# One core, a Macaron block (two top-1 MoE layers around a circulant state-space layer): order of the w1 load and its centering, square roots through Ln and Exp, slot softmax ahead of the third expert's output copy, last expert's rows written straight into row form

## The chip, the cores and the metric

One core of one Trainium2 chip (trn2). The metric is the device time of one execution in microseconds (us). The kernel before took 154.5 us in the median of three runs (153.84 to 155.39).

## The reference

The input `x` is 8 x 512 tokens of 128 floats. `LN` is a layer norm without gain and bias, epsilon 1e-5.

```python
x = x + 0.5 * moe(LN(x))          # first pass
x = x + ssm(LN(x))
x = x + 0.5 * moe(LN(x))          # second pass

def moe(tokens):                  # 4096 tokens, E = 8 experts, F = 512, CAP = 160
    probs = softmax(tokens @ gate_w)
    expert = argmax(probs)
    pos = running count of the token within its expert; dropped when pos >= CAP
    return probs[expert] * (relu(tokens @ w1[expert]) @ w2[expert])   # 0 for a dropped token

def ssm(u):                       # per batch, state h of 128
    h_t = W h_(t-1) + B_w u_t     # W circulant, diagonal in the Fourier basis, |eigenvalue| 1
    return C_w h_t + D * u_t
```

## The kernel before

All arithmetic is float32 apart from the counting masks. The program has three stages, and five engines that run their own instruction lists and meet through semaphores.

**Head (0 to 32 us).** PE computes gate logits of all tokens from a transposed copy of x (`gate_turned`, `turn_logits`). DVE picks the expert of each token (`rate`, `choose`, L575 to L586), counts (`count_up`, L614), PE turns counts into ranks with three small matmuls (`rank`, L923 to L926), DVE makes one-hot tables (`number`, `encode`, `encode_place`, L630 to L656), and PE multiplies them, 32 matmuls of 20 columns (`place`, L934), which gives the list of tokens by slot (`index` on DVE, L664 to L671, tile `tok`). There are 8 x 160 = 1280 slots, in 10 tiles of 128. In between PE centers w1: the layer norm's mean is folded into the weights by a 128 x 128 product per expert (`center_w1`, L907, PSUM banks 0 and 1 in turn, copied back to `w1s` by ScalarE, L398). `keep_warm` (L863) are dummy bf16 matmuls of 512 columns. The constants, x, w1 and w2 come in one after the other on SyncE's queue (L265 to L277): w1 and w2 in halves, each half of w1 (1024 KB) followed by the same experts' w2.

**A MoE pass (`slots(n)`, first 32 to 61 us, second 117 to 153 us).** GpSimd issues ten gathers, one for each tile of slots (`gather`, L326), each row by token number. PE turns each gathered tile (step `i`, L949), ScalarE copies it to `xcT` (L406), and PE computes slot logits (`l`, L954), the first product of an expert (`u`, L965, four chunks in two halves, ReLU by ScalarE, L414) and the second (`d`, L976), which comes out transposed. DVE copies that to `eoT` (L705), PE turns it to rows (`o`, L985), DVE scales it by the slot's probability and adds the residual (`xnew`, L715), and GpSimd scatters the tile (L335). The probabilities need the variances of all ten tiles (`gmv`, L679), a root (`gsd`, L423, Sqrt), the reciprocal `grs` (L684), three DVE instructions to `lg`, an Exp (`prob_e`, L427) and three more DVE instructions to `gscale` (L694 to L696). Sqrt and Exp lie in different activation tables, so a table is loaded at L424 in each pass, ahead of the Exp, and one at L459 for the state-space stage.

The order inside a pass is written out by hand in three strings, one for each of PE, DVE and ScalarE: in `pe_steps` `u3` is expert 3's first product, in `dve_steps` `d2` its copy of expert 2's output, `l0` and `f0` the two halves of the softmax; in `act_steps` `g0` is the root, `e0` the Exp, `u` the ReLUs.

**State-space stage (61 to 108 us).** Eight batches go through a ring between ScalarE and PE: `normalise` (u, L466), `turn_u` (L1034), `copy_uT` (L453), `group_sums` (L1043), `turned_part` (vq, L445 and L446), and again `normalise` of the batch two further. Beside it DVE computes statistics (`stats`, L737 and L742), `shift` (L753 and L754) and the recurrence (va, z, zs, state), GpSimd two products of it. `deviation(b)` (L459, Sqrt) gives the standard deviation `ssd`, whose reciprocal `srs` DVE makes in `shift`; `ssd` itself scales the gate logits for the second pass (`gate_back`, L798). The second pass's ranks, places and index are computed in the last batches (L575 to L671 again), and its gathers wait for the index and for the last write of x2.

ScalarE's list at the start of this stage, and the layer norm's root:

```python
deviation(0); normalise(0); deviation(1); copy_uT(0); normalise(1); turned_part(0)
for i in range(NB):
    copy_uT(i + 1); deviation(i + 2); turned_part(i + 1); normalise(i + 2)
```

Of the kernel before, what the change touches and what calls it, by code (L numbers as in the profile page):

```python
# [5 lines left out]
def macaron_moe_ssm_kernel(nc, x_in, x_turned, a_params, b_w, c_w, c_w_turned, d_skip, gate_w, w1, w2,  # L6
# [40 lines left out]
    with ctx:  # L47
# [171 lines left out]
        gsd_r, lg_r, pe_r = (sem(n) for n in ("gsd_r", "lg_r", "pe_r"))  # L219
# [2 lines left out]
        svar, ssd_r, snb_r, u_r = (sem(n) for n in ("svar", "ssd_r", "snb_r", "u_r"))
# [30 lines left out]
        pe_steps = steps("i0 x1 i1 x2 u0 i2 l0 l1 d0 i3 u1 i4 u2 i5 d1 i6 l2 l3 i7 l4 l5 u3 i8 l6 l7 i9 l8 l9 d2 "  # L253
                         "u4 o0 o1 d3 u5 o2 o3 d4 o4 u6 o5 d5 u7 o6 d6 o7 d7 o8 o9")

        dve_steps = steps("i0 i1 i2 i3 i4 d0 i5 i6 i7 i8 d1 i9 l0 d2 f0 o0 o1 d3 p5 "
                          "o2 o3 d4 p6 o4 o5 d5 o6 d6 o7 d7 o8 o9")

        act_steps = steps("i0 i1 u0 i2 i3 u1 i4 u2 i5 i6 i7 u3 i8 i9 g0 e0 u4 u5 u6 u7")
# [928 lines left out]
```

## Time and profile before

| | |
|---|---|
| median of 3 runs | 154.5 us (153.84 to 155.39) |
| the profiled execution's own time | 155.39 us |
| its span, first to last instruction | 153.2 us |
| PE busy | 135.3 us (88%) |
| DVE, ACT (ScalarE), POOL (GpSimd) busy | 88.6, 57.4, 54.3 us |
| mean granted TensorE clock | 0.956 of full speed |
| half clock granted in | slices 6 and 7 of 40 (around 23 to 31 us), slice 30, and the end |

A matmul of float32 operands stands as two rows (two passes), so an expert's product of 4 chunks is "x8". PEld is the loading of stationary operands, which overlaps PE. In a row of the timeline the first number is the start, the second the time that it covers, then engine, line, operation, output and input tiles; `pair` is a PSUM pair of banks. In square brackets stands how long the engine was idle before it and who released it. SPq and POOLq are the instruction queues of SyncE and GpSimd. A span on POOL is rough.

### The profile page before, as it was taken

How to read it: one execution, taken by the hardware profiler on the slowest of the kernel's cores; microseconds unless marked ns; L12 is line 12 of the kernel's file. 1: busy time of each engine (PE TensorE's matmuls, PEld its weight loads, DVE VectorE, ACT ScalarE, POOL GpSimd, SP SyncE). 2: the span in 40 equal slices, each digit the busy share in tenths (PEclk: the TensorE clock that was granted, in tenths of full speed). 3: DMA queues.
4: the chain of work that ended last, by engine and by line, in shares of the span. 5: the costliest groups of instructions: out<-in, count | busy, mean ns of one | idle time of the engine just before them, and what ended most of it. 6: DMA issues, size and time to landing. Idle time of an engine off the chain costs nothing.

```text
span 153.2 us, 2526 instructions
## 1 busy us (share of the span) xinstructions
PE 135.3 (88%) x784; PEld 103.0 (67%) x784; DVE 88.6 (58%) x384; ACT 57.4 (37%) x141; POOL 54.3 (35%) x87
## 2 busy tenths in 40 slices
PE   5897999999999969579999999999979899999810
PEld 2324476368999946239888778878874399899700
DVE  1078796954446541276877978999882243554220
ACT  2513410444583406055564656451100145742200
POOL 3440000777205777101311221122002777027770
PEclk9999995599999999999999999999996999999995
DMA  4999999111100111690011011101011111001110
GB/s 121 282 357 386 369 486 415 39 51 51 34 0 17 58 51 54 199 327 28 0 68 45 23 73 68 70 1 68 4 68 68 51 51 51 21 0 51 54 51 17
DMA packets 11308, 16.21 MB, mean 106 GB/s; under 512 B 1664, under 2 KB 6272, under 8 KB 11264
## 3 DMA queue, kind: packets, MB, share of 16 engines
q1 hardware_dynamic: 9504, 13.11, 24.2%
q0 software_dynamic: 1280, 2.62, 5.5%
q10 hardware_dynamic: 512, 0.33, 0.9%
q8 instruction: 6, 0.10, 0.3%
q14 instruction: 6, 0.05, 0.1%
HBM read 12.65 MB, written 5.51 MB: 118 GB/s over the span
## 4 chain that ended last, share of the span: by engine, by line
PE 43%; issue 12%; DVE 11%; DMA 11%; POOL 10%; ACT 5%; SPq 4%; POOLq 1%; DVEq 0%
PE pair L965 9%; PE pair L976 7%; PE pair L907 7%; DMA w1s<-w 5%; POOL xg L326 4%; PE pair L1043 4%; ACT u L466 3%; SPq L267 2%; PE pair L934 2%; POOL out L335 2%; PE pair L863 2%; POOL x_scratch L335 2%; PE pair L1034 2%; DMA x<-x_scratch 2%; DVE sstat L737 2%
## 5 line engine op out<-in xcount | busy, mean ns | idle before, releaser
L863 PE MATMUL pair<-warm_in,ones_bf 128*128 128x512 bf16 x70 | 20.3, 437 | 3.3 <-DMA x<-x_scratch 1.7
L976 PE MATMUL pair<-hT,w2s 128*128 128x160 f32 x128 | 20.4, 302 | 0.2 <-ACT hT L414 0.2
L965 PE MATMUL pair<-xcT,w1s 128*128 128x160 f32 x128 | 20.5, 303 | 0.0
L414 ACT ACTIVATE hT<-pair 128x320 f32<-128x320 f32 x32 | 14.0, 438 | 15.2 <-PE pair L965 13.5
L965 PEld LDWEIGHTS pair<-xcT,w1s 128*128 128x128 f32 x128 | 18.0, 190 | 1.2 <-ACT xcT L406 0.8
L976 PEld LDWEIGHTS pair<-hT,w2s 128*128 128x128 f32 x128 | 17.9, 190 | 0.4 <-issue 0.2
L326 POOL DMA_INDIRECT xg<-x,tok x10 | 10.2, 1020 | 19.9 <-issue 19.9
L863 PEld LDWEIGHTS pair<-warm_in,ones_bf 128*128 128x128 bf16 x70 | 7.5, 112 | 13.1 <-issue 4.7
L326 POOL DMA_INDIRECT xg<-out,tok x10 | 10.1, 1012 | 13.6 <-DVE tok L671 10.8
L678 DVE BATCH_NORM_STATS2 gstat<-xg 128x6 f32<-128x128 f32 x20 | 5.8, 290 | 14.2 <-DMA xg<-out,tok 10.3
L335 POOL DMA_INDIRECT x_scratch<-xnew,tok x10 | 9.9, 993 | 10.8 <-DVE xnew L715 9.0
L335 POOL DMA_INDIRECT out<-xnew,tok x10 | 9.9, 990 | 9.4 <-DVE xnew L715 7.2
L356 POOL TENSOR_TENSOR vb<-vq,st 128x128 f32<-128x128 f32 x8 | 3.7, 458 | 25.9 <-ACT vq L446 25.9
L466 ACT ACTIVATE u<-x,snb,srs 128x128 f32<-128x128 f32 x28 | 11.6, 482 | 0.7 <-DVE snb L754 0.5
L406 ACT COPY xcT<-pair 128x128 f32<-128x128 f32 x20 | 5.3, 264 | 15.9 <-PE pair L949 15.8
L907 PE MATMUL pair<-w1s,center 128*128 128x512 f32 x16 | 10.5, 806 | 0.2 <-DMA w1s<-w 0.2
L705 DVE COPY eoT<-pair 128x160 f32<-128x160 f32 x16 | 5.1, 318 | 8.2 <-PE pair L976 8.2
L715 DVE SCALAR_TENSOR_TENSOR xnew<-pair,gscale,xg 128x128 f32<-128x128 f32 x20 | 6.4, 347 | 5.9 <-PE pair L985 5.9
L1043 PE MATMUL pair<-uT,vt 128*128 128x128 f32 x64 | 8.5, 276 | 0.9 <-ACT uT L453 0.9
L737 DVE BATCH_NORM_STATS2 sstat<-x 128x6 f32<-128x128 f32 x32 | 6.9, 278 | 3.8 <-DMA x<-x_scratch 3.8
L398 ACT COPY w1s<-pair 128x512 f32<-128x512 f32 x8 | 4.7, 586 | 11.6 <-PE pair L907 11.6
L1077 PE MATMUL pair<-gt,state 128*128 128x272 f32 x32 | 8.8, 396 | 0.0
(181 smaller groups left out, 245.0 us busy)
## 6 DMA issues: line engine op xcount, KB each, us to landing
xt<-x_turned SPq DMA_DIRECT2D x8, 256.0 KB, 5.9
w1s<-w SPq DMA_DIRECT2D x2, 1024.0 KB, 7.4
w2s<-w SPq DMA_DIRECT2D x8, 256.0 KB, 6.7
x<-x_scratch SPq DMA_DIRECT2D x8, 256.0 KB, 4.3
out<-x SPq DMA_DIRECT2D x8, 256.0 KB, 2.0
ce<-const_early ACTq DMA_DIRECT2D x1, 318.0 KB, 4.7
...
xg<-x,tok POOLq DMA_INDIRECT x10, 2.5
```

The source lines that it names most:

```text
L326: pool.indirect_dma_start(xg[:, j, :], None, (x_rows, out_rows)[n], bass.IndirectOffsetOnAxis(ap=tok[:, j:j + 1], axis=0), bounds_check=T ...
L335: pool.indirect_dma_start((x1_dram, out_rows)[n], bass.IndirectOffsetOnAxis(ap=tok[:, j:j + 1], axis=0), xnew[:, j, :], None, bounds_check ...
L414: nc.scalar.activation(hT[:, e % 2, half * HC:(half + 1) * HC, :], bank[4 + half][:, 0:HC * CAP] .rearrange("p (c s) -> p c s", c=HC), ACT ...
L466: ins = nc.scalar.activation(u[:, b % 2, c, :], x1[:, b * TB + c, :], ACT.Identity, bias=snb[:, b % 2, c:c + 1], scale=srs[:, b % 2, c:c + 1])
L715: V.scalar_tensor_tensor(xnew[:, i, :], bank[2 + i % 2][:, 0:P], gscale[:, i:i + 1], xg[:, i, :], ALU.mult, ALU.add).then_inc(row_sb, 1)
L737: ins = V.bn_stats(sstat[:, b % 2, c, :], x1[:, b * TB + c, :])
L863: M(bank[to][:, :], ones_bf[:, :], warm_in[:, :], start=True, stop=True)
L907: M(bank[e % 2][:, :], center[:, :], w1s[:, e, :], start=True, stop=True).then_inc(w1c_ps, 1)
L965: ins = M(bank[4 + half][:, c * CAP:(c + 1) * CAP], w1s[:, i, ch * P:(ch + 1) * P], xcT[:, i * CAP:(i + 1) * CAP], start=True, stop=True)
L976: ins = M(bank[6 + i % 2][:, 0:CAP], w2s[:, i, c, :], hT[:, i % 2, c, :], start=(c == 0), stop=(c == FC - 1))
L1043: ins = M(bank[5][:, 0:NG], vt[:, TB - 1 - c, :], uT[:, b % 2, c * P:(c + 1) * P], start=(c == 0), stop=(c == TB - 1))
L1077: ins = M(y[:, h, E:E + 2 * PITCH], state[:, b % 2, :], gt[:, 2 * h:2 * h + 2, :].rearrange("p r c -> p (r c)"), start=False, stop=True, s ...
```

## The change

1. SyncE issues both halves of w1 before all of w2.
2. On PE, experts 4 and 5 of w1 are centered ahead of `place(0, 0)`, experts 6 and 7 behind it. Eight `keep_warm` matmuls that stood ahead of `place` are gone.
3. Roots are taken as exp(0.5 ln v), and reciprocal roots as exp(-0.5 ln v), on ScalarE. One table with Ln and Exp is loaded at the start. The reciprocals of DVE at L684 and L753 are gone. The state-space stage has three activations for each batch instead of one.
4. In a pass `u3` goes behind `i9 l8 l9` on PE; `o0 o1` go ahead of `u4`; on ScalarE the root goes ahead of `u3`'s ReLUs, the Exp behind them; on DVE `f0` goes ahead of `d2`.
5. Expert 7's second product takes hT as the stationary operand and w2 as the moving one (step `t`), so it comes out in rows: `t8` (32 slots) and `t9` (128 slots) replace `d7`, DVE's copy of it, `o9` and a part of `o8`.
6. In `choose`, the last instruction writes `chosen` in its own order (expert, then tile) and reads `key` across.

```diff
             for i in range(2):
                 h = slice(i * E // 2, (i + 1) * E // 2)
                 sp.dma_start(w1s[:, h, :], w1[h].rearrange("e d f -> d e f")).then_inc(d_w1[i], 16)
+            for i in range(2):
                 for e in range(i * E // 2, (i + 1) * E // 2):
                     sp.dma_start(w2s[:, e, :, :], w2[e].rearrange("(c p) d -> p c d", p=P)).then_inc(d_w2[i], 16)
...
-            nc.scalar.activation(table_load[:, 0:1], eps[:, 0:1], ACT.Sqrt)
+            nc.scalar.preload_act_table_set("natural_log_exp_and_others")
...
-                        act.wait_ge(rated, n * NS + NS)
-                        nc.scalar.activation(gsd[:, :], gmv[:, :, 1], ACT.Sqrt, bias=eps[:, 0:1]).then_inc(gsd_r, 1)
-                        nc.scalar.activation(table_load[:, 1:2], eps[:, 0:1], ACT.Exp)
+                        act.wait_ge(rated, n * NS + g1)
+                        nc.scalar.activation(gln[:, g0:g1], gmv[:, g0:g1, 1], ACT.Ln, bias=eps[:, 0:1]).then_inc(gln_r, 1)
+                        act.wait_ge(gln_r, group(n, i) + 1)
+                        nc.scalar.activation(grs[:, g0:g1], gln[:, g0:g1], ACT.Exp, scale=-0.5).then_inc(grs_r, 1)
...
             def deviation(b):
                 act.wait_ge(svar, b + 1)
+                nc.scalar.activation(sln[:, b % 2, :], smv[:, b % 2, :, 1], ACT.Ln, bias=eps[:, 0:1]).then_inc(sln_r, 1)
+                act.wait_ge(sln_r, b + 1)
+                if 2 <= b < 4:
+                    act.wait_ge(u_half, b - 1)
+                nc.scalar.activation(srs[:, b % 2, :], sln[:, b % 2, :], ACT.Exp, scale=-0.5).then_inc(srs_r, 1)
                 if b >= 4:
                     act.wait_ge(y_read, b - 3)
-                nc.scalar.activation(ssd[:, b % 4, :], smv[:, b % 2, :, 1], ACT.Sqrt, bias=eps[:, 0:1]).then_inc(ssd_r, 1)
+                nc.scalar.activation(ssd[:, b % 4, :], sln[:, b % 2, :], ACT.Exp, scale=0.5).then_inc(ssd_r, 1)
...
-                return V.tensor_tensor(chosen[n][k][:, :, t0 - first:t0 - first + wd].rearrange("p e t -> p t e"),
-                                       key[:, ts, :], top_key[:, ts].unsqueeze(2).broadcast_to([P, wd, E]), ALU.is_equal)
+                return V.tensor_tensor(chosen[n][k][:, :, t0 - first:t0 - first + wd],
+                                       key[:, ts, :].rearrange("p t e -> p e t"),
+                                       top_key[:, ts].unsqueeze(1).broadcast_to([P, E, wd]), ALU.is_equal)
...
-                link(V.reciprocal(srs[:, b % 2, :], ssd[:, b % 4, :]))
...
+                    elif kind == "t":
+                        s0, s1 = max((E - 1) * CAP, i * P), (i + 1) * P
+                        pe.wait_ge(h_sb, n * 2 * E + 2 * E)
+                        pe.wait_ge(row_sb, n * NS + i - 1)
+                        for c in range(FC):
+                            ins = M(bank[2 + i % 2][s0 - i * P:P, 0:D],
+                                    hT[:, (E - 1) % 2, c, s0 - (E - 1) * CAP:s1 - (E - 1) * CAP], w2s[:, E - 1, c, :],
+                                    start=(c == 0), stop=(c == FC - 1), skip_group_check=True)
+                        if s0 == i * P:
+                            ins.then_inc(row_ps, 1)
...
             center_w1(0, 2)
             rank(0, 0)
-            center_w1(2, E // 2)
+            center_w1(2, E - 2)
+            place(0, 0)
+            center_w1(E - 2, E)
             pe.wait_ge(gg_sb, 1)
-            keep_warm(8, 4)
-            place(0, 0)
-            center_w1(E // 2, E)
             keep_warm(4, 4)
             slots(0)
```

In the head, PE's list from the first two centered experts on reads before:

```order
L907 MATMUL pair<-w1s,center 128x512 x2
L923 MATMUL pair<-counted_0,before_bf 128x256
L924 MATMUL pair<-counted_0,after_bf 128x8x28
L926 MATMUL pair<-counted_0,ident_bf 128x256
L907 MATMUL pair<-w1s,center 128x512 x2
L863 MATMUL pair<-warm_in,ones_bf 128x512 x8
L934 MATMUL pair<-hot_tok,hot_place 64x20 x32
L907 MATMUL pair<-w1s,center 128x512 x4
L863 MATMUL pair<-warm_in,ones_bf 128x512 x4
L949 MATMUL pair<-ce,xg 128x128
```

and after (L935 is the centering, L962 `place`, L891 `keep_warm`):

```order
L935 MATMUL pair<-w1s,center 128x512 x2
L951 MATMUL pair<-counted_0,before_bf 128x256
L952 MATMUL pair<-counted_0,after_bf 128x8x28
L954 MATMUL pair<-counted_0,ident_bf 128x256
L935 MATMUL pair<-w1s,center 128x512 x4
L962 MATMUL pair<-hot_tok,hot_place 64x20 x32
L935 MATMUL pair<-w1s,center 128x512 x2
L891 MATMUL pair<-warm_in,ones_bf 128x512 x4
L977 MATMUL pair<-ce,xg 128x128
```

Two experts have moved ahead of `place` and eight dummy matmuls are gone. In a pass, PE's list from the turning of tile 7 on reads before (L949 turns a gathered tile, L954 slot logits, L965 `u`, L976 `d`, L985 `o`):

```order
L949 MATMUL pair<-ce,xg 128x128
L954 MATMUL pair<-gate_c,xcT 128x8 x2
L965 MATMUL pair<-xcT,w1s 128x160 x4
L949 MATMUL pair<-ce,xg 128x128
L954 MATMUL pair<-gate_c,xcT 128x8 x2
L949 MATMUL pair<-ce,xg 128x128
L954 MATMUL pair<-gate_c,xcT 128x8 x2
L976 MATMUL pair<-hT,w2s 128x160 x4
L965 MATMUL pair<-xcT,w1s 128x160 x4
L985 MATMUL pair<-ce,eoT 128x128 x2
L976 MATMUL pair<-hT,w2s 128x160 x4
```

and after (in the same order L977, L982, L993, L1004, L1024):

```order
L977 MATMUL pair<-ce,xg 128x128
L982 MATMUL pair<-gate_c,xcT 128x8 x2
L977 MATMUL pair<-ce,xg 128x128
L982 MATMUL pair<-gate_c,xcT 128x8 x2
L977 MATMUL pair<-ce,xg 128x128
L982 MATMUL pair<-gate_c,xcT 128x8 x2
L993 MATMUL pair<-xcT,w1s 128x160 x4
L1004 MATMUL pair<-hT,w2s 128x160 x4
L1024 MATMUL pair<-ce,eoT 128x128 x2
L993 MATMUL pair<-xcT,w1s 128x160 x4
L1004 MATMUL pair<-hT,w2s 128x160 x4
```

Expert 3's first product has moved behind tile 9 and its logits; the turning of the first two output tiles has moved ahead of expert 4's. ScalarE's list from the last slot copies of the first pass to the first batch of the state-space stage reads before (xcT slot copies, hT ReLUs):

```order
L406 COPY xcT<-pair 128x128 x2
L423 ACTIVATE gsd<-gmv,eps 128x10
L424 ACT_TABLE_LOAD
L424 ACTIVATE table_load<-eps 128x1
L427 ACTIVATE prob_e<-lg 128x80
L414 ACTIVATE hT<-pair 128x320 x8
L434 COPY vt<-pair 128x512
L436 COPY tab<-pair 128x136
L437 COPY tab<-pair 128x272
L459 ACT_TABLE_LOAD
L459 ACTIVATE ssd<-smv,eps 128x4
```

and after:

```order
L420 COPY xcT<-pair 128x128 x5
L438 ACTIVATE gln<-gmv,eps 128x10
L440 ACTIVATE grs<-gln 128x10
L428 ACTIVATE hT<-pair 128x320 x2
L444 ACTIVATE prob_e<-lg 128x80
L428 ACTIVATE hT<-pair 128x320 x8
L451 COPY vt<-pair 128x512
L453 COPY tab<-pair 128x136
L454 COPY tab<-pair 128x272
L474 ACTIVATE sln<-smv,eps 128x4
L478 ACTIVATE srs<-sln 128x4
L481 ACTIVATE ssd<-sln 128x4
```

Both table loads are gone, one expert's ReLUs stand between the root and the Exp, and each deviation is three activations.

## Rows read from the trace of the kernel before

**Rows 1.** Page, part 4: the chain that ended last, by engine.

```profile
PE 43%; issue 12%; DVE 11%; DMA 11%; POOL 10%; ACT 5%; SPq 4%; POOLq 1%; DVEq 0%
```

**Rows 2.** The same chain in order of time: start us, us, what; one expert's product.

```profile
50.79 1.09 PE pair L976 x8
```

**Rows 3.** Windows of the head: busy time by engine, then granted clock.

```profile
23.50:24.00 0.50, 0.50 (x7) 0.50 (x6) 0.00 (x0) 0.00 (x0) 0.00 (x0) 0.65 0.00 0
...
30.00:30.50 0.50, 0.50 (x1) 0.10 (x1) 0.47 (x3) 0.49 (x1) 0.35 (x1) 0.52 0.01 0
```

**Rows 4.** Timeline of the head, PE: centering, warm-up, place, centering.

```profile
17.32 1.88 PE L907 MATMUL pair<-w1s,center 128*128 128x512 f32 x4
...
19.04 1.89 PE L863 MATMUL pair<-warm_in,ones_bf 128*128 128x512 bf16 x8
...
20.86 3.70 PE L934 MATMUL pair<-hot_tok,hot_place 128*64 128x20 f16 x32
...
24.48 6.67 PE L907 MATMUL pair<-w1s,center 128*128 128x512 f32 x8
```

**Rows 5.** Line L274, the two loads of w1: issue times and landing.

```profile
L274 SPq DMA_DIRECT2D w1s<-w x2: 434/1100/1767, 7.6 to 13.4; - x2
...
DMA to landing us min/median/max: 7.3/7.4/7.5
```

**Rows 6.** Timeline of the first pass, 41 to 48 us.

```profile
41.01 0.29 DVE L678 BATCH_NORM_STATS2 gstat<-xg 128x6 f32<-128x128 f32 x1 [0.64 <-DMA xg<-x,tok]
...
42.46 0.31 PE L949 MATMUL pair<-ce,xg 128*128 128x128 f32 x1
...
43.29 1.28 ACT L424 ACT_TABLE_LOAD   x1
...
43.36 1.33 PE L976 MATMUL pair<-hT,w2s 128*128 128x160 f32 x8
...
44.69 0.25 ACT L427 ACTIVATE prob_e<-lg 128x80 f32<-128x80 f32 x1
...
45.28 0.98 ACT L414 ACTIVATE hT<-pair 128x320 f32<-128x320 f32 x2 [0.33 <-PE pair L965]
...
46.00 0.61 DVE L715 SCALAR_TENSOR_TENSOR xnew<-pair,gscale,xg 128x128 f32<-128x128 f32 x2 [0.33 <-PE pair L985]
...
47.23 1.02 POOL L335 DMA_INDIRECT x_scratch<-xnew,tok  x1 [7.75 <-DVE xnew L715]
```

**Rows 7.** Timeline of the first pass's end: last two tiles and their scatters.

```profile
56.80 0.61 DVE L715 SCALAR_TENSOR_TENSOR xnew<-pair,gscale,xg 128x128 f32<-128x128 f32 x2 [0.42 <-PE pair L985]
...
57.92 0.98 POOL L335 DMA_INDIRECT x_scratch<-xnew,tok  x1 [0.60 <-DVE xnew L715]
...
59.21 0.98 POOL L335 DMA_INDIRECT x_scratch<-xnew,tok  x1 [0.31 <-issue]
```

**Rows 8.** Waits: engine, line, waited for, us in total, times, longest us.

```profile
PE pair L985 <- DVE eoT L705: 1.7, 4, 0.4
```

**Rows 9.** Timeline at the start of the state-space stage, ScalarE.

```profile
68.11 0.30 ACT L459 ACTIVATE ssd<-smv,eps 128x4 f32<-128x4 f32 x1 [0.96 <-DVE smv L742]
68.32 0.57 ACT L453 COPY uT<-pair 128x512 f32<-128x512 f32 x1
```

**Rows 10.** Timeline inside the ring, ScalarE.

```profile
78.83 0.26 ACT L445 COPY vq<-pair 64x128 f32<-64x128 f32 x1 [1.29 <-PE pair L1043]
```

**Rows 11.** Timeline at the end of the stage: gate tables, expert choice.

```profile
106.03 1.00 PE L1095 MATMUL pair<-tg,uT 128*128 128x64 f32 x8
...
107.22 0.41 PE L1101 MATMUL pair<-gt,state 128*128 128x32 f32 x2 [0.19 <-DVE state L783]
...
109.34 0.70 DVE L586 TENSOR_TENSOR chosen<-key,top_key 128x128 bf16<-128x128 bf16 x1
```

**Rows 12.** Timeline of the second pass: tile 9, first and last scatter.

```profile
131.85 0.29 DVE L678 BATCH_NORM_STATS2 gstat<-xg 128x6 f32<-128x128 f32 x1 [0.55 <-DMA xg<-out,tok]
...
136.64 1.02 POOL L335 DMA_INDIRECT out<-xnew,tok  x1 [6.25 <-DVE xnew L715]
...
148.67 0.98 POOL L335 DMA_INDIRECT out<-xnew,tok  x1 [0.31 <-issue]
```

More of the change, by code:

```diff
@@ L218, in macaron_moe_ssm_kernel @@
         rated, slotT_ps, slotT_sb, slot_logits = (sem(n) for n in ("rated", "slotT_ps", "slotT_sb", "slot_logits"))
[L219 removed]
+        gln_r, grs_r, lg_r, pe_r = (sem(n) for n in ("gln_r", "grs_r", "lg_r", "pe_r"))
         h_ps, h_sb, eo_ps, eo_sb, row_ps, row_sb = (sem(n) for n in ("h_ps", "h_sb", "eo_ps", "eo_sb", "row_ps",
                                                                      "row_sb"))
[L222 removed]
+        svar, sln_r, srs_r, ssd_r, snb_r, u_r = (sem(n) for n in ("svar", "sln_r", "srs_r", "ssd_r", "snb_r", "u_r"))
         uT_ps, uT_sb, v_ps, vq_sb, va_r, vb_r, z_r = (sem(n) for n in ("uT_ps", "uT_sb", "v_ps", "vq_sb", "va_r",
@@ L249, in steps, with group @@
             return [(word[0], int(word[1])) for word in text.split()]
[L253 to L259, printed above, removed]
+        GROUPS = [[(0, NS)], [(0, NS)]]
+        def group(n, i):
+            return n * len(GROUPS[0]) + i
+        pe_steps = [steps("i0 x1 i1 x2 u0 i2 l0 l1 d0 i3 u1 i4 u2 i5 d1 i6 l2 l3 i7 l4 l5 i8 l6 l7 "
+                         "i9 l8 l9 u3 d2 o0 o1 u4 d3 u5 o2 o3 d4 o4 u6 o5 d5 u7 o6 d6 t8 o7 o8 t9"),
+                    steps("i0 x1 i1 x2 u0 i2 l0 l1 d0 i3 u1 i4 u2 i5 d1 i6 l2 l3 i7 l4 l5 i8 l6 l7 "
+                         "i9 l8 l9 u3 d2 o0 o1 u4 d3 u5 o2 o3 d4 o4 u6 o5 d5 u7 o6 d6 t8 o7 o8 t9")]
+        dve_steps = [steps("i0 i1 i2 i3 i4 d0 i5 i6 i7 i8 d1 i9 l0 f0 d2 "
+                         "o0 o1 d3 p5 o2 o3 d4 p6 o4 o5 d5 o6 d6 o7 o8 o9"),
+                    steps("i0 i1 i2 i3 i4 d0 i5 i6 i7 i8 d1 i9 l0 f0 "
+                         "d2 o0 o1 d3 o2 o3 d4 o4 o5 d5 o6 d6 o7 o8 o9")]
+        act_steps = [steps("i0 i1 u0 i2 i3 u1 i4 u2 i5 i6 "
+                         "i7 i8 i9 g0 u3 e0 u4 u5 u6 u7"),
+                    steps("i0 i1 u0 i2 i3 u1 i4 u2 i5 i6 "
+                         "i7 i8 i9 g0 u3 e0 u4 u5 u6 u7")]
         block = ctx.enter_context(nc.Block())
@@ L416, in relu @@
                                              .rearrange("p (c s) -> p c s", c=HC), ACT.Relu).then_inc(h_sb, 1)
-                for kind, i in act_steps:
+                for kind, i in act_steps[n]:
                     if kind == "i":
@@ L939, in slots @@
             def slots(n):
-                for kind, i in pe_steps:
+                for kind, i in pe_steps[n]:
                     if kind == "x":
@@ L984, in slots @@
                             pe.wait_ge(row_sb, n * NS + i - 1)
-                        nc.tensor.transpose(bank[2 + i % 2][:, 0:P], eoT[:, i * P:(i + 1) * P], ident)\
+                        s1 = min((i + 1) * P, (E - 1) * CAP)
+                        nc.tensor.transpose(bank[2 + i % 2][0:s1 - i * P, 0:P], eoT[:, i * P:s1], ident)\
                             .then_inc(row_ps, 1)
```

58 lines of the change are left out of this document (33 added, 25 removed).

## The prediction

> **What bounds the kernel.** I read the chain that ended last first. PE has 43% of it [rows 1], but PE is 88% busy, so the question is in each stage which wait ends last. I then read the timeline stage by stage.
>
> In the head PE is never idle, but part of its work is filler: eight dummy matmuls of 1.89 us in all stand ahead of `place`, and eight rows of centering behind it take 6.67 us where four took 1.88 [rows 4]. That is the clock: in the window 23.5 to 24.0 the granted share is 0.65 and in 30.0 to 30.5 it is 0.52 [rows 3], so it fell from 2.4 to 1.2 GHz at 23.65 and rose at 30.48. What comes next needs the index, which only follows `place`. The gathers then pace the pass.
>
> In the first pass the reader should compare two times: tile 9 reaches DVE at 41.01, but PE turns it at 42.46, because expert 3's first product stands ahead of tiles 8 and 9 in its list [rows 6]. The softmax needs all ten tiles, so Exp comes at 44.69, the first output tile at 46.00 and the first scatter at 47.23 [rows 6]. From then on GpSimd is the bound: one scatter in 1.29 us (57.92 to 59.21) [rows 7]. Ten of them without a pause would put the last at 47.23 + 9 x 1.29 = 58.84. It stands at 59.21, so 0.37 us were lost, at tile 8, where POOL was idle for 0.60 waiting for `xnew` instead of its usual 0.31 [rows 7]. So a pass ends with the later of two things: the first scatter plus 11.6 us, or the last output tiles plus their scatters.
>
> In the second pass tile 9 reaches DVE at 131.85, and the scatters run from 136.64 to 148.67 [rows 12]. PE was not late there: landing to first scatter is 4.79 us, against 6.22 in the first pass.
>
> In the state-space stage the ring is ScalarE and PE. ScalarE stands idle for 1.29 us ahead of the vq copies [rows 10].
>
> **The change, part by part.**
>
> *Queue and head.* No byte is added. The second half of w1 was issued at 13.4 and needs 7.3 us to land, so it came at 20.7; the first came at 7.6 + 7.5 = 15.1 [rows 5]. Moved ahead of 1 MB of w2, it should land one transfer behind the first, (20.7 - 15.1) / 2 = 2.8 us later, at 17.9. w2's first half comes that much later, and is needed only for the first expert's second product, behind two gathers. PE wants expert 4 at 19.04, where the dummies start [rows 4]. Two experts take 1.88 us against the dummies' 1.89, so `place` starts within 0.1 us of 20.86; I take +0.1. Its four tables from DVE are ready either way. The drop of the clock I leave where it is. Behind `place` two experts cost half of 6.67, 3.3 us, and four dummies at half clock twice 4 x 0.24, 1.9 us. PE is then ready for tile 0 at 24.6 + 3.3 + 1.9 = 29.8; before it was at 24.5 + 6.7 + 1.0 = 32.1. The pass becomes bound by the gathers.
>
> *First pass.* With `u3` behind tile 9, PE can turn it at 41.05 + 0.1 for the later index. Let me leave the 0.1 out and add it at the end. Tile 9 to the next product was 43.36 - 42.46 = 0.90, so `u3` starts at 41.95. A product takes 1.09 [rows 2]; one that began at 43.36 + 1.09 = 44.45 had its ReLUs at 45.28 for 0.98, so they end 1.81 behind its start [rows 6]: 43.76. The root is done by then (on ScalarE it stands ahead of these ReLUs), and so is `lg`. Exp takes 0.25, to 44.0. From the end of Exp to `xnew` it was 46.00 - 44.94 = 1.06; now three small DVE instructions and the copy of `d2` stand there, which I price the same: 45.07. The scatter came 1.23 behind: 46.30, 0.93 earlier. Ten scatters end at 46.30 + 11.61 = 57.91 instead of 59.21: **-1.30**.
>
> This needs tile 8 in time. PE went from `d2` (43.36) to tile 8's `xnew` (56.80) in 13.44 us. The new list has ten products there as before. It loses two waits for `eoT` of 0.42 (four in two passes) [rows 8], which `t8` now covers, and gains `t8`, 128 columns instead of 160, 1.09 x 0.8 = 0.87. So it takes 13.47 from 41.95: 55.42, done at 55.75. Scatter 8 is due at 46.30 + 8 x 1.29 = 56.62 and was 0.78 behind its tile where POOL waited (57.13 to 57.92, the first of two in 0.61), so the tile is wanted at 55.84. It just holds. `t9` waits for tile 7's `xnew` and has 1.3 us more. With the 0.1 of the head the first pass gives **-1.2**.
>
> *The table loads.* The one at 43.29 took 1.28 [rows 6] and Exp went off at 44.69, 0.12 behind its end; the other lies in a wait for DMA. Both vanish, but the Exp now waits for ReLUs instead, so the saving is already in the sum and not on top.
>
> *State-space stage.* `deviation(1)` stands ahead of `copy_uT(0)`, which waits for nothing else: 68.11 to 68.32 [rows 9]. The Sqrt itself is 0.30 long. Now three activations stand there. Ln takes 0.30 and its own wait some 0.05 before Exp can start. An Exp of 80 elements took 0.25 [rows 6] and one overlaps its follower by 0.09 (68.11 + 0.30 - 68.32), so each adds at most 0.16: 0.35 + 0.32 - 0.21 = 0.46. From below an Exp of 4 elements costs no less than a third of that, 0.25 in all. I take +0.4, nearest to the Exp row. Queued behind it is only the ring, which starts that much later.
>
> The Trainium skill ("ScalarE: Activation LUTs", section "What ACT_TABLE_LOAD costs") gives an activation without a pointer operand 186 ns plus 0.833 ns per element, and 93 ns of overlap; by that the step would be 0.33 instead of 0.4, an estimate that no row here shows for 4 elements.
>
> Inside the ring the two extra activations, at most 0.46, fit into the 1.29 us of idle time [rows 10]: nothing. If that cover were gone, six batches would pay up to 0.46 each. The reciprocals that DVE loses there are not in the ring either.
>
> At the end of the stage DVE took over: L1101 waited 0.19 for DVE's state at 107.22, while L1095 ended at 107.03 [rows 11]. The late ring pushes L1095 by 0.4, DVE gains by `chosen` and the reciprocals, so L1101 comes 0.2 later. The `chosen` of 0.70 us [rows 11] runs over 128 elements; the statistics of DVE over as many took 0.29 [rows 6]. Written in order I give it 0.3, between 0.2 and the old 0.7. That gives 0.4 back, if PE is free for the ranks. PE still has the last batch's matmuls then, so I count a small part of it: **+0.1** for the stage, between -0.8 and +0.4.
>
> *Second pass.* The same steps from tile 9: its landing is 131.85 - 41.01 = 90.84 later, so the first scatter comes at 46.30 + 90.84 = 137.14, **0.5 later** than before, since here PE wasn't late and `u3`'s ReLUs now stand ahead of Exp. But the pause at tile 8 is gone: 137.14 + 11.61 = 148.75 against 148.67: **+0.1**. `d7`'s copy and `o9` are off the path, which is what pays.
>
> Sum: -1.2 + 0.1 + 0.1 = -1.0. The profiled execution took 155.39 (span 153.2 and 2.2 around it), so it would take 154.4. It is 0.9 above the median, so I set the median to 154.5 - 1.0 = **153.5 us**.
>
> **Rivals.**
> A, DVE's savings count in full. For it: the chain of the last batches is mostly DVE's, with `chosen` in it twice. Against: PE and the vq copies stand ready only just ahead. Twice 0.4 off and nothing for the ring: -0.8 instead of +0.1, 152.6 us.
>
> B, the first pass behaves like the second: PE reaches tile 9 no earlier (a slower `place`, copies by ScalarE queued behind ReLUs) and the ReLUs ahead of Exp cost their 0.5. Then it is +0.1 in each of three places: 154.8. Against it stands 1.4 us of lateness at 42.46.
>
> C, slower: the clock. The head issues less to PE: eight dummies gone, and pauses behind 29.8, where PE waits for tiles 0 and 1. If 1.2 GHz stays past 30.48, PE falls behind the gathers. It starts 2.3 us earlier and has a product less before tile 9, and was 1.4 late: 2.3 + 1.1 - 1.4 = 2.0 spare, used up by 4 us at half clock. From 34.5 on each us costs half a us. Held to the last gather at 41, that is +3.3: 156.8. For it: after the fall PE was busy without a pause for 6.8 us until the clock rose. Against: that includes the slow part of `place`. The Trainium skill ("TensorE: Matmul & The Clock Gate", section "What's actually happening") makes sustained activity the thing that releases the gate; by that the pauses speak for C.
>
> D, w1's second half lands at 20.7 as before, as if the reordering did nothing. Then `place` waits behind expert 5 until 20.7 + 1.9 = 22.6 instead of 20.9, +1.7: 155.2.
>
> **Chances.** Forecast 0.50 (152.6 to 154.1), A 0.20, B 0.17, C 0.07, D 0.06. One per cent, 1.5 us, is about what a measurement of this kernel can tell from no change. Below 152.95 lie most of A and a fifth of the forecast: 0.29. Above 156.05 lie C and what B and D leave over: 0.13. The range 151.9 to 155.6 leaves C out, and a little of A.
>
> **What would show it.** Right: w1's second half lands near 18; `place` starts at 20.9 to 21.1; tile 9 is turned within 0.2 of its landing; first scatter 5.3 behind tile 9 in both passes; no pause at tile 8; uT of batch 0 starts 0.4 later behind the statistics; the ring's period unchanged. Wrong: a PE wait for w1 ahead of `place`, a clock of 0.5 behind 31 us, scatters with pauses, or ScalarE busy right up to vq.

## The result and the profile after

| | before | after |
|---|---|---|
| median | 154.48 us (4 runs, 153.84 to 155.39) | 159.54 us (4 runs, 159.15 to 160.76) |
| ratio | | 1.035, interval 1.031 to 1.040: slower |
| profiled execution, span | 155.39, 153.2 us | 159.36, 157.6 us |

The forecast was 153.5, the range ended at 155.6. I take the stages in the prediction's order. First the head: timeline of PE, as [rows 4].

```profile
17.01 3.75 PE L935 MATMUL pair<-w1s,center 128*128 128x512 f32 x8
20.69 3.70 PE L962 MATMUL pair<-hot_tok,hot_place 128*64 128x20 f16 x32
24.32 2.77 PE L935 MATMUL pair<-w1s,center 128*128 128x512 f32 x4
26.88 1.91 PE L891 MATMUL pair<-warm_in,ones_bf 128*128 128x512 bf16 x4
29.31 0.33 PE L977 MATMUL pair<-ce,xg 128*128 128x128 f32 x1 [0.52 <-DMA xg<-x,tok]
```

Eight rows of centering run without a wait, `place` starts at 20.69 instead of 20.86, and PE is done with its filler at 26.88 + 1.91 = 28.8 and waits for tile 0. The clock was at half from 25.38 for 3.41 us. Both halves of w1 were issued by 8.2, and the slower took 9.1 us (lines view, L287, as [rows 5]), so it was there at 17.3:

```profile
L287 SPq DMA_DIRECT2D w1s<-w x2: 532/636/740, 7.5 to 8.2; - x2
...
DMA to landing us min/median/max: 7.3/8.2/9.1
```

Events come in the order of the forecast, 0.3 to 1.0 us ahead of its times. Then the first pass, windows of one us, with the columns us, PE, PEld, DVE, ACT, POOL, granted clock, DMA share, GB/s:

```profile
38.00:39.00 1.00, 1.00 (x12) 1.00 (x11) 0.48 (x2) 0.37 (x2) 0.70 (x2) 1.00 0.25 61
39.00:40.00 1.00, 0.55 (x6) 0.46 (x6) 0.33 (x2) 0.17 (x1) 0.31 (x1) 1.00 0.02 4
40.00:41.00 1.00, 0.40 (x5) 0.31 (x4) 0.43 (x3) 0.27 (x1) 0.00 (x0) 1.00 0.24 66
41.00:42.00 1.00, 0.78 (x6) 0.69 (x7) 0.40 (x2) 0.66 (x3) 0.00 (x0) 1.00 0.00 0
42.00:43.00 1.00, 1.00 (x7) 1.00 (x7) 0.72 (x3) 0.24 (x2) 0.00 (x0) 0.72 0.00 0
43.00:44.00 1.00, 1.00 (x6) 1.00 (x5) 0.00 (x0) 0.37 (x2) 0.00 (x0) 0.50 0.00 0
44.00:45.00 1.00, 1.00 (x6) 1.00 (x5) 0.46 (x3) 0.44 (x2) 0.00 (x0) 0.50 0.00 0
45.00:46.00 1.00, 1.00 (x6) 0.96 (x6) 0.17 (x1) 0.00 (x0) 0.00 (x0) 0.57 0.08 16
```

PE is busy for 0.55, 0.40 and 0.78 of the three windows around tiles 8 and 9, and at 42.45 the clock falls to 1.2 GHz for 3.41 us, just where PE's work sets the pace. The timeline of the same stretch, against [rows 6]:

```profile
40.92 0.29 DVE L701 BATCH_NORM_STATS2 gstat<-xg 128x6 f32<-128x128 f32 x1 [0.57 <-DMA xg<-x,tok]
...
40.94 0.33 PE L977 MATMUL pair<-ce,xg 128*128 128x128 f32 x1 [0.60 <-DMA xg<-x,tok]
...
41.63 0.39 PE L982 MATMUL pair<-gate_c,xcT 128*128 128x8 f32 x2 [0.22 <-ACT xcT L420]
...
41.87 1.94 PE L993 MATMUL pair<-xcT,w1s 128*128 128x160 f32 x8
...
43.60 2.34 PE L1004 MATMUL pair<-hT,w2s 128*128 128x160 f32 x8
...
43.85 0.44 ACT L428 ACTIVATE hT<-pair 128x320 f32<-128x320 f32 x1 [0.63 <-PE pair L993]
44.18 0.26 ACT L444 ACTIVATE prob_e<-lg 128x80 f32<-128x80 f32 x1
```

Tile 9 is turned 0.02 behind its landing and `u3` starts at 41.87 (forecast 41.95). But `u3` covers 1.94 us, `d2` 2.34 (it was 1.33), and Exp comes at 44.18. The scatters of the first pass, against [rows 7]:

```profile
47.51 1.02 POOL L349 DMA_INDIRECT x_scratch<-xnew,tok  x1 [8.20 <-DVE xnew L742]
48.83 1.00 POOL L349 DMA_INDIRECT x_scratch<-xnew,tok  x1 [0.30 <-issue]
50.79 0.98 POOL L349 DMA_INDIRECT x_scratch<-xnew,tok  x1 [0.95 <-DVE xnew L742]
...
57.85 0.98 POOL L349 DMA_INDIRECT x_scratch<-xnew,tok  x1 [0.93 <-DVE xnew L742]
...
60.43 0.98 POOL L349 DMA_INDIRECT x_scratch<-xnew,tok  x1 [0.30 <-issue]
```

The first stands 6.59 behind tile 9, and there are two new pauses: POOL idle for 0.95 ahead of the scatter of tile 2 and for 0.93 ahead of tile 7's, instead of 0.30. The second pass does the same (timeline, against [rows 12]; the clock is at half from 134.61 for 3.41 us):

```profile
133.48 0.29 DVE L701 BATCH_NORM_STATS2 gstat<-xg 128x6 f32<-128x128 f32 x1 [0.49 <-DMA xg<-out,tok]
...
140.04 1.02 POOL L349 DMA_INDIRECT out<-xnew,tok  x1 [8.05 <-DVE xnew L742]
...
143.29 0.98 POOL L349 DMA_INDIRECT out<-xnew,tok  x1 [0.93 <-DVE xnew L742]
...
150.42 0.98 POOL L349 DMA_INDIRECT out<-xnew,tok  x1 [1.01 <-DVE xnew L742]
...
153.00 0.98 POOL L349 DMA_INDIRECT out<-xnew,tok  x1 [0.30 <-issue]
```

In the state-space stage, ScalarE ahead of batch 0's uT, the ring, DVE's `chosen`, PE's product behind it and the second pass's first gather (timelines, against [rows 9 to 11]):

```profile
69.55 0.30 ACT L474 ACTIVATE sln<-smv,eps 128x4 f32<-128x4 f32 x1 [0.95 <-DVE smv L769]
69.88 0.20 ACT L478 ACTIVATE srs<-sln 128x4 f32<-128x4 f32 x1
69.99 0.19 ACT L481 ACTIVATE ssd<-sln 128x4 f32<-128x4 f32 x1
70.09 0.57 ACT L470 COPY uT<-pair 128x512 f32<-128x512 f32 x1
...
75.58 0.26 ACT L462 COPY vq<-pair 64x128 f32<-64x128 f32 x1 [0.90 <-PE pair L1081]
...
111.10 0.39 DVE L608 TENSOR_TENSOR chosen<-key,top_key 128x128 bf16<-128x128 bf16 x1
...
111.40 1.03 PE L1124 MATMUL pair<-x,ce 128*128 128x256 f32 x4
...
119.14 1.11 POOL L340 DMA_INDIRECT xg<-out,tok  x1 [10.69 <-DVE tok L694]
```

The last scatter moved from 148.67 to 153.00, +4.33: tile 9 -0.09, from it to the first pass's last scatter +1.30 (18.20 to 19.50), from there to the second pass's tile 9 +0.41, from it to the last scatter +2.71 (16.81 to 19.52), taken before rounding. So 4.0 of 4.3 us stand between tile 9 and the last scatter of the two passes.

### The profile page after: what moved, and what is told of

It reads as the page before. It is cut to its first block, busy times and chain, and to the rows that moved or that the text cites. A ratio compares the mean times of both kernels' runs of the same rounds, so it can differ in the third digit from the quotient of the medians.

```text
span 157.6 us, 2543 instructions
## 1 busy us (share of the span) xinstructions
PE 137.2 (87%) x790; PEld 105.8 (67%) x790; DVE 85.1 (54%) x372; ACT 55.9 (35%) x153; POOL 54.3 (34%) x87
## 4 chain that ended last, share of the span: by engine, by line
PE 43%; issue 15%; POOL 13%; DMA 11%; DVE 7%; ACT 5%; POOLq 1%; SPq 1%; DVEq 0%
POOL xg L340 8%; PE pair L993 8%; PE pair L1004 8%; PE pair L1081 4%; DMA xt<-x_turned 4%; PE pair L935 3%; ACT u L488 3%; PE pair L962 2%; PE pair L914 2%; PE pair L1072 2%; PE pair L1103 2%; PE pair L1105 2%; DMA x<-x_scratch 2%; DMA xg<-x,tok 2%; DVE sstat L764 2%
## 5 line engine op out<-in xcount | busy, mean ns | idle before, releaser
L993 PE MATMUL pair<-xcT,w1s 128*128 128x160 f32 x128 | 22.1, 319 | 0.0
L891 PE MATMUL pair<-warm_in,ones_bf 128*128 128x512 bf16 x62 | 19.1, 457 | 3.3 <-DMA x<-x_scratch 1.7
L993 PEld LDWEIGHTS pair<-xcT,w1s 128*128 128x128 f32 x128 | 19.2, 201 | 1.2 <-ACT xcT L420 0.8
L1004 PE MATMUL pair<-hT,w2s 128*128 128x160 f32 x112 | 19.5, 322 | 0.2 <-ACT hT L428 0.2
L1004 PEld LDWEIGHTS pair<-hT,w2s 128*128 128x128 f32 x112 | 17.6, 209 | 0.4 <-issue 0.2
L891 PEld LDWEIGHTS pair<-warm_in,ones_bf 128*128 128x128 bf16 x62 | 7.0, 118 | 12.5 <-issue 5.2
L977 PE MATMUL pair<-ce,xg 128*128 128x128 f32 x20 | 6.0, 298 | 3.9 <-DMA xg<-x,tok 2.2
L732 DVE COPY eoT<-pair 128x160 f32<-128x160 f32 x14 | 4.4, 315 | 8.3 <-PE pair L1004 8.3
L1081 PEld LDWEIGHTS pair<-uT,vt 128*128 128x128 f32 x64 | 7.8, 191 | 1.5 <-ACT uT L470 1.5
```

The source lines that it names most:

```text
L891: M(bank[to][:, :], ones_bf[:, :], warm_in[:, :], start=True, stop=True)
L977: nc.tensor.transpose(bank[i % 2][:, 0:P], xg[:, i, :], ident)\
L993: ins = M(bank[4 + half][:, c * CAP:(c + 1) * CAP], w1s[:, i, ch * P:(ch + 1) * P], xcT[:, i * CAP:(i + 1) * CAP], start=True, stop=True)
L1004: ins = M(bank[6 + i % 2][:, 0:CAP], w2s[:, i, c, :], hT[:, i % 2, c, :], start=(c == 0), stop=(c == FC - 1))
L1081: ins = M(bank[5][:, 0:NG], vt[:, TB - 1 - c, :], uT[:, b % 2, c * P:(c + 1) * P], start=(c == 0), stop=(c == TB - 1))
```

## The experiments

Two theories. **K**: by moving `u3`, the change opens waits on PE ahead of tiles 8 and 9, and the clock falls because of them. **S**: the order and the new steps cost by themselves: `o0 o1` ahead of `u4` leave three products (`u4 d3 u5`) between the turning of tiles 1 and 2, hence the pause at tile 2; `t8` ahead of `o7` makes the pause at tile 7; `u3`'s ReLUs stand ahead of Exp. In all that follows "first" and "last" are starts of the first and last scatter behind tile 9's statistics, first pass / second pass, from each run's timeline. A stretch at half clock is given by its start and length; those at the very end, behind 147 us, are left out. "Inside a pass" means behind the turning of its first tile: between the stage and the second pass, while PE waits for the index, every run has one such stretch (in the changed kernel 117.54, 3.41 us; tile 0 is turned at 121.90), and these are named only where the text needs them. The kernel before, run again beside these, had medians of 154.15 to 154.2 us. The edits of the step strings are shown in part.

### Undoing one thing in the changed kernel

Dummies in the waits (step `y2` is two dummy matmuls, `y1` one; each step waits for ReLUs that are long done):

```diff
-l4 l5 i8 l6 l7 i9 l8 l9 u3
+l4 l5 y2 i8 l6 l7 y2 i9 y1 l8 l9 u3
+                    elif kind == "y":
+                        pe.wait_ge(h_sb, n * 2 * E + 6)
+                        keep_warm(i)
```

> The changed kernel, with five dummy matmuls of 512 bf16 columns on PE where it waits for tiles 8 and 9 and for the last slot copy (two, two and one, 1.1 us in all, as long as the product of expert 3 that was moved away from there). No order changes. Theory K (clock): the half clock granted at 42.45 and 134.61, for 3.41 us each, follows from those waits. With dummies it stays at 1.0, PE gets back half of 3.41 us in each pass, and all of it is on the path: first scatter near 46.3 instead of 47.51, last scatter of a pass 1.7 us earlier, in all -3.4 us: about 156.1 us. Theory S (spacing of the output tiles): POOL's pauses at tiles 2 and 7 set the end of the pass, whatever PE's clock, so below 1 us comes back: about 159 us.

Measured 155.89 us (ratio 1.012, 1.009 to 1.015). First 5.13 / 5.09, last 17.82 / 17.85; half clock only at 23.64 and 115.80, 3.41 us each, none inside a pass. K holds: with more work on PE the kernel is 3.65 us faster, 1.68 and 1.67 in the passes, half of 3.41. The pauses stay.

`u3` and its ReLUs back in their old place, all else as changed:

```diff
-l4 l5 i8 l6 l7 i9 l8 l9 u3 d2
+l4 l5 u3 i8 l6 l7 i9 l8 l9 d2
-i7 i8 i9 g0 u3 e0 u4
+i7 u3 i8 i9 g0 e0 u4
```

> The changed kernel with expert 3's first product ahead of tiles 8 and 9 again on PE, its ReLUs ahead of them on ScalarE, and Exp directly behind the root. All else as changed. Theory K: no half clock in the passes, and no ReLUs ahead of Exp. Tile 9 can still be turned when it lands, at 40.9, so the product behind it starts at 41.9 instead of 42.9 of warm time: first scatter near 45.5, last near 57.8 (60.43 now, 59.21 before). In all -2.6 us in each pass, 154.3 us. If the clock is not the cause but the ReLUs ahead of Exp are, it brings 0.5 in each pass: 158.5. If it is about the same as the run with the dummies (156.1), the moved product costs nothing but the clock.

153.94 us (0.999, 0.996 to 1.001). First 4.50 / 4.46, last 16.79 / 16.80; half clock at 24.18 for 3.41 us and, between stage and second pass, at 112.93 for 6.83, none inside a pass; the pause at tile 2 is gone, the one at tile 7 stays (1.91 and 1.99 from scatter to scatter instead of 1.29). This one step takes back all of the loss. Of its 5.6 us the filled run shows 3.65 as the clock's; the other 1.95 (1.04 and 1.05 in the passes) are the order's, which is theory S's share.

`o0 o1` back behind `u4`, and, in another kernel, `o7` ahead of `t8`:

```diff
-u3 d2 o0 o1 u4 d3
+u3 d2 u4 o0 o1 d3
```

> The changed kernel with the turning of output tiles 0 and 1 behind expert 4's first product again. Theory S: between tiles 0 and 2 now stand three products (3.3 us) where scatters want 2 x 1.29, so the early first scatter only becomes a pause of 0.95 at tile 2. Put back, the first scatter comes 0.9 later and the pause goes: 159.5 us, no difference within 0.3. The other theory, that the first scatter sets the end of the pass: +0.9 in each pass, 161.3 us.

160.71 us (1.042, 1.039 to 1.045), 1.2 more than expected. In the second pass the pause at tile 2 is gone, and the first scatter is 0.90 later for it (7.46); last 19.51, unchanged. In the first pass the clock was at half for 6.83 us from 40.88, and last is 20.83. So, as the second pass shows, `o0 o1` only decide where PE's lateness comes out. That the 1.2 us over the changed kernel come from the longer half clock of the first pass is read from this one trace (last 1.33 later there), not tested.

```diff
-o6 d6 t8 o7 o8 t9
+o6 d6 o7 t8 o8 t9
```

> The changed kernel with output tile 7 turned ahead of step t8. Theory S: t8 (1.0 us) ahead of tile 7 makes the pause of 0.93 and 1.01 us in POOL's scatters at tile 7. Turned first, PE waits 0.5 us for DVE's copy of expert 6, but tile 7 comes 0.6 us earlier, tiles 8 and 9 are in time, and the last scatter comes 0.6 us earlier in each pass: -1.2, 158.3 us. Rival: PE's tail is what counts, and its wait for the copy is added: +0.5 in each pass, 160.5 us.

156.52 us (1.015, 1.012 to 1.018), 3.0 less than as changed, where 1.2 was expected. In the second pass last is 19.01, 0.51 less, as S says (0.6 expected). In the first pass it is 17.32: no fall there, though the step can't touch the waits for tiles 8 and 9. In this execution the head's half clock came at 29.61 instead of 25.38. That was unexplained, so:

> The changed kernel once more, unchanged. Open is whether the falls of the clock inside the passes (42.45 and 134.61 in the changed kernel, but none in the first pass of the run with o7 ahead of t8, whose waits for tiles 8 and 9 are the same) belong to the kernel or to the phase of one execution. Theory 'the kernel's order decides': 159.5 us again, with a fall of 3.41 us near 42.5 and one near 134.6. Rival 'phase': the falls stand elsewhere or one is missing, and the time differs from 159.5 by 1.7 us for each fall more or less.

159.91 us (1.039, 1.031 to 1.047). The same time, from other places: half clock 29.62+3.41 in the head, none in the first pass (last 17.83), 132.02+6.83 in the second (last 21.02). Windows of the first pass of this execution, against those above:

```profile
39.00:40.00 1.00, 1.00 (x11) 1.00 (x11) 0.37 (x2) 0.27 (x1) 0.33 (x1) 1.00 0.02 4
40.00:41.00 1.00, 0.97 (x11) 0.88 (x10) 0.43 (x3) 0.53 (x2) 0.00 (x0) 1.00 0.27 66
41.00:42.00 1.00, 0.78 (x6) 0.69 (x7) 0.36 (x2) 0.68 (x3) 0.00 (x0) 1.00 0.00 0
```

A half clock from 29.6 to 33.0 made PE late, so PE was still catching up at tile 8: busy 1.00 and 0.97 instead of 0.55 and 0.40. Most of the waits were gone, and there was no fall (another reading stands in the last section). And in its second pass PE was busy for 0.59, 0.45 and 0.78 of 130 to 133 us, and the clock fell at 132.02. The place of a fall differs between executions of one kernel, so one trace doesn't show where another execution has them. Of the eight executions of these two sets, five have spans of 157.1 to 157.9 and a mean clock of 0.942 to 0.950, three have 159.0 or 159.1 and 0.929 to 0.932: the step, about 1.6, fits the 1.7 us of one stretch, though only two of the eight have a trace.

Both remedies together:

```diff
-l4 l5 i8 l6 l7 i9 l8 l9 u3
+l4 l5 y2 i8 l6 l7 y2 i9 y1 l8 l9 u3
...
-d6 t8 o7 o8 t9
+d6 o7 t8 o8 t9
```

> o7 ahead of t8 and, besides, five dummy matmuls in PE's waits for tiles 8 and 9. K (the clock falls because PE waits there): no fall in either pass, so last scatter 17.82 - 0.5 = 17.3 behind tile 9 in both passes; against the filled run (155.9 us) 0.5 off in each pass: 154.9 us. Rival (the o7 step itself kept the clock up in the first pass, and the dummies do nothing more): second pass still with a fall, last scatter 19.0 behind tile 9, 156.5 us.

154.91 us (1.006, 1.004 to 1.008). First 5.13 / 5.09, last 17.33 / 17.34, no fall inside a pass. Against the filled run 0.50 and 0.51 came back, so the clock and `t8`'s place add up.

### Doing one thing to the kernel before

```diff
-l4 l5 u3 i8 l6 l7 i9 l8 l9 d2
+l4 l5 i8 l6 l7 i9 l8 l9 u3 d2
-i6 i7 u3 i8 i9 g0 e0 u4
+i6 i7 i8 i9 g0 u3 e0 u4
```

> The kernel before with one edit: u3 behind i9 l8 l9 on PE, its ReLUs between root and Exp on ScalarE. K (the waits for tiles 8 and 9 that this opens let the clock fall): a half clock of 3.4 us or more within 2 us behind tile 9 in each pass where PE was in time before it; first scatter 6.9 instead of 5.2 behind tile 9, last 18.6; two passes 154.2 + 3.6 = 157.8 us. Rival (order and row form of the other edits are needed for the loss): first scatter 5.2, last 17.0 behind tile 9: 154.6 us.

159.71 us (1.037, 1.030 to 1.043): this one step is worth the whole loss, 1.9 more than K's 157.8. First 7.57 / 7.54, last 19.55 / 19.57; half clock at 42.21 and 134.37, 3.41 us each. Its windows:

```profile
40.00:41.00 1.00, 0.68 (x5) 0.59 (x5) 0.68 (x3) 0.27 (x1) 0.00 (x0) 1.00 0.28 66
41.00:42.00 1.00, 0.53 (x4) 0.44 (x4) 0.48 (x2) 0.39 (x2) 0.00 (x0) 1.00 0.00 0
42.00:43.00 1.00, 1.00 (x5) 1.00 (x6) 0.72 (x4) 0.98 (x2) 0.00 (x0) 0.61 0.00 0
```

The same with the five dummies (edit as above):

> The same and five dummy matmuls in the waits for tiles 8 and 9. K: no fall in the passes, first scatter 5.2 behind tile 9, last 17.0: 154.6 us, 3.2 less than without the dummies. Rival (the loss is in the order, not in the clock): as without them, or more, since PE has more to do.

156.18 us (1.012, 1.007 to 1.018). First 5.90 / 5.87, last 17.88 / 17.90, no fall inside a pass (nor in the head of this execution). The windows:

```profile
40.00:41.00 1.00, 0.98 (x7) 0.49 (x6) 0.52 (x3) 0.27 (x1) 0.00 (x0) 1.00 0.27 66
41.00:42.00 1.00, 0.92 (x7) 0.79 (x7) 0.55 (x3) 0.55 (x3) 0.00 (x0) 1.00 0.00 0
42.00:43.00 1.00, 1.00 (x9) 1.00 (x9) 0.83 (x4) 1.00 (x1) 0.00 (x0) 1.00 0.00 0
```

Of the 5.6 us of `u3`'s step the clock is 3.5. The other 2.0 are order: in the second pass 1.09 (first 5.87 against 4.78; both theories had named 5.2). The timelines of the second pass, first of the kernel before (tile 9 at 131.85), then of this one (tile 9 at 131.50):

```profile
134.13 0.25 ACT L427 ACTIVATE prob_e<-lg 128x80 f32<-128x80 f32 x1
...
134.94 0.17 DVE L696 SCALAR_TENSOR_TENSOR gscale<-grs,prob_rc 128x10 f32<-128x10 f32 x1
```

```profile
134.41 0.27 ACT L427 ACTIVATE prob_e<-lg 128x80 f32<-128x80 f32 x1
...
134.91 0.33 DVE L705 COPY eoT<-pair 128x160 f32<-128x160 f32 x1 [1.42 <-PE pair L979]
...
135.66 0.17 DVE L696 SCALAR_TENSOR_TENSOR gscale<-grs,prob_rc 128x10 f32<-128x10 f32 x1
```

Exp starts 2.91 behind tile 9 (before: 134.13 - 131.85 = 2.28), because the table load stands ahead of `u3`'s ReLUs and they ahead of Exp. The last step of the softmax starts 4.16 behind it (before: 134.94 - 131.85 = 3.09): `d2`'s copy still stands ahead of the softmax's second half on DVE, and `d2` now comes behind `u3`. So 0.63 is the Exp's and the rest the copy's, a reading of this trace that no run tested. In the changed kernel `f0` goes ahead of `d2`, which avoids the second part.

The head alone:

```diff
-            center_w1(2, E // 2)
+            center_w1(2, E - 2)
+            place(0, 0)
+            center_w1(E - 2, E)
             pe.wait_ge(gg_sb, 1)
-            keep_warm(8, 4)
-            place(0, 0)
-            center_w1(E // 2, E)
             keep_warm(4, 4)
```

(and both halves of w1 ahead of w2).

> The kernel before with the head's part of the change alone (both halves of w1 first, centering of experts 4 and 5 ahead of place, eight dummies gone). If the head's step gives what the forecast said of it (the clock falls for 3.4 instead of 6.8 us, PE ready at 29.8 instead of 32.1 and in time for tile 9): first pass as the second of before, last scatter about 17 behind tile 9 instead of 18.20: -1.2 to -1.4, 153.0 us. Rival: the pauses ahead of tiles 0 and 1 let the clock fall in the first pass, +1.7 from there: 154.5 to 156 us.

154.28 us (0.998, 0.995 to 1.001): nothing, where 153.0 was expected. Yet its first pass is what was forecast, last 16.79, though its clock was at half for 6.83 us from 23.45. A gain of 1.4 in the trace and none in the median suggests that the trace of before was not a usual execution. So once more the kernel before:

> The kernel before once more, unchanged, for a second trace. The trace that the forecast was read from has a span of 153.2 us; of 25 later executions 19 lie between 151.6 and 152.7 and 6 between 153.0 and 153.5. Theory: the first pass's lateness (tile 9 turned 1.4 late, last scatter 18.20 behind tile 9) belonged to that execution alone, whose clock was at half for 6.83 us in the head; in a usual execution the half clock stands elsewhere, the last scatter of the first pass is 16.8 behind tile 9 as in the second, and the span is 151.8. Rival: 18.2 again in the first pass, and the 1.4 us are saved in the second pass or in the state-space stage.

154.34 us, and this trace is of the same kind: half clock 23.20+6.83, first pass 6.12 and 18.09, second 4.78 and 16.81, span 153.0. The other kind shows in the numbers of the runs. Of 57 executions of before beside my experiments, 10 have a mean clock of 0.955 or 0.956, as the first trace has, and spans of 152.7 to 153.5; the other 47 have other clocks, 0.949 to 0.980, and spans of 151.5 to 152.5. What a usual first pass probably looks like is shown by the next kernel, whose head has the same steps: a half clock of 3.41 us there, and last 17.02. A trace of before itself in such an execution I did not get, so that its first pass is in time there is inferred from spans and clocks, not seen.

The roots alone (Ln and Exp in the passes and in `deviation`, reciprocals gone, the order of steps as before):

```diff
-                        nc.scalar.activation(gsd[:, :], gmv[:, :, 1], ACT.Sqrt, bias=eps[:, 0:1]).then_inc(gsd_r, 1)
-                        nc.scalar.activation(table_load[:, 1:2], eps[:, 0:1], ACT.Exp)
+                        nc.scalar.activation(gln[:, :], gmv[:, :, 1], ACT.Ln, bias=eps[:, 0:1]).then_inc(gln_r, 1)
+                        act.wait_ge(gln_r, n + 1)
+                        nc.scalar.activation(grs[:, :], gln[:, :], ACT.Exp, scale=-0.5).then_inc(grs_r, 1)
...
```

> The kernel before with the roots alone: Ln and Exp for Sqrt, no table load in the passes, three activations for each batch, the reciprocals of DVE gone; order of the steps as before. Theory: the load of 1.28 us ran beside DVE's work on the logits, so the first scatter comes only 0.3 earlier behind tile 9 (4.5 instead of 4.8) and the last one not at all, since tile 8 is PE's; the first uT comes 0.33 later: 154.2 + 0.3 = 154.5 us. Rival: each load of 1.28 us was on the path: 151.6 us.

154.04 us (0.998, 0.995 to 1.002): nothing, as forecast, but the first scatter did not come 0.3 earlier either: 4.78 in the second pass, as before. Its Exp starts 2.0 behind tile 9, but on DVE `d2`'s copy still stands ahead of the rest of the softmax, which is ready at 134.6 us, and PE turns tile 0 only behind `u4`, at the same moment:

```profile
133.40 0.27 ACT L428 ACTIVATE prob_e<-lg 128x80 f32<-128x80 f32 x1 [0.92 <-DVE lg L694]
133.50 1.25 PE L971 MATMUL pair<-xcT,w1s 128*128 128x160 f32 x8
...
134.58 0.38 PE L991 MATMUL pair<-ce,eoT 128*128 128x128 f32 x2
```

### A version that beats both

The changed kernel, `u3` and its ReLUs back, `o7` ahead of `t8`, and batch 0's uT ahead of batch 1's deviation:

```diff
-i8 l6 l7 i9 l8 l9 u3 d2 o0 o1 u4 ... d6 t8 o7 o8 t9
+u3 i8 l6 l7 i9 l8 l9 d2 o0 o1 u4 ... d6 o7 t8 o8 t9
             normalise(0)
-            deviation(1)
             copy_uT(0)
+            deviation(1)
```

> The changed kernel with u3 and its ReLUs back ahead of tile 8, o7 ahead of t8, and batch 0's uT copied ahead of batch 1's deviation. The u3 step alone gave 153.9 us with first and last scatter 4.5 and 16.8 behind tile 9; the pause at tile 7 (1.92 to 1.99 instead of 1.29) should shrink to 1.45, 0.5 off in each pass, and the first uT comes 0.33 earlier: 152.7 us. Rival: the ring or the index hides the 0.33, and the pause moves to tile 8 instead of shrinking: 153.9 us.

152.76 us (0.990, 0.988 to 0.993). First 4.51 / 4.46, last 16.28 / 16.29, half clock only at 24.29 and 113.03, 3.41 us each. It is 1% below the kernel before, clear of the interval. The scatters of its second pass (timeline of POOL) run almost without a pause:

```profile
134.48 1.01 POOL L349 DMA_INDIRECT out<-xnew,tok  x1 [6.01 <-DVE xnew L742]
...
143.74 0.98 POOL L349 DMA_INDIRECT out<-xnew,tok  x1 [0.50 <-issue]
...
146.31 0.98 POOL L349 DMA_INDIRECT out<-xnew,tok  x1 [0.30 <-issue]
```

## Why the prediction was wrong

**Head: right.** w1's second half 17.3 (17.9 forecast), `place` at 20.69 (20.96), PE ready at 28.8 (29.8): `place` began 0.27 earlier, and the clock fell at 25.38 and not at 23.65, so a part of the centering that began at 24.32 still ran at 2.4 GHz (2.77 instead of 3.3). The four dummies took 1.91 at 1.2 GHz, as forecast. Rival D fell with it (`place` did not wait), and so did B's mechanism (tile 9 was turned at once).

**First pass, the first scatter: right but for the clock.** "With `u3` behind tile 9" the first scatter was to come 5.29 behind it. With the waits filled it came 5.13 and 5.09 behind it; as changed, 6.59 and 6.56.

**The step that failed first: the clock inside the passes.** I let PE become bound by the gathers ("The pass becomes bound by the gathers") and counted no price for it. In the kernel before, `u3` was not only work that made PE late, it also filled PE's wait for tiles 8 and 9. Rival C named the clock, but held it in the head and put the danger at PE falling behind the gathers; the fall came where PE was ahead of them. Its 156.8 and its 0.07 were both too small. Cost: 1.7 us in each pass, shown by two pairs of kernels (159.54 to 155.89, 159.71 to 156.18) that differ in dummies alone. The Trainium skill ("TensorE: Matmul & The Clock Gate", section "HAM oscillation — how this bites in real kernels") describes a clock that falls through PE's waits for DMA. The trace agrees in kind, but its waits were much shorter than those of the page's example: PE's longest single wait ahead of the fall at 42.45 was 0.60 us.

**Second: "Ten of them without a pause".** I checked tile 8 alone. Tile 8 did hold, but tile 2 and tile 7 came late, by 0.4 and 0.6 us in the filled run (17.82 against 16.90 forecast, although the first scatter was 0.16 earlier). For tile 7 the cause is `t8` ahead of `o7`, shown: 0.5 back in each pass. For tile 2 it is the three products ahead of it, shown in the second pass; undone, the pause goes but the first scatter is later and the last one stays at 19.51.

**Third: setting the median by the difference.** "I set the median to 154.5 - 1.0" took over a first pass that was 1.4 late only in about one execution of six, going by the runs' spans and clocks. If the usual first pass is like the second, my own sum gives +0.1 there: the forecast would have been that of rival B, +0.3, not -1.0. The head alone measured it: 154.28. Together, 0.3, 3.4 for the clock and 1.9 for the pauses less the earlier first scatter (0.92 and 0.95 in the filled run against 16.90) make 5.6 us; measured were 5.3 over 154.2.

**State-space stage.** From the start of batch 1's three activations to uT it is 70.09 - 69.55 = 0.54 instead of 0.21, so +0.33, not 0.4. The Trainium skill's figures ("ScalarE: Activation LUTs", section "What ACT_TABLE_LOAD costs") gave 0.33 as the estimate, and the rows of 0.20 and 0.19 for 4 elements agree with them. The ring's period stayed 5.02. `chosen` took 0.39, not the forecast 0.30. Rival A, DVE's savings in full, was off: uT of batch 0 came 1.77 later than before and L1139 1.76 later than L1101 (108.98 against 107.22), so the reciprocals gave nothing up to there. Of the 0.31 that `chosen` saved, some 0.15 reached the gathers (119.14 against 117.53, +1.61), since PE was busy with L1124 until 112.4. From batch 1's deviation (+1.44) to the gathers the stage thus lost 0.2; the rest of the 0.41 lies ahead of it.

**Second pass.** First scatter +0.31 for the ReLUs ahead of Exp, as the filled run has it (0.5 forecast), plus the clock and the pauses: +2.71 instead of +0.1.
